# Final norm of a state-space plus expert block: who gathers, who normalises, and in which buffers, during the last expert

## The chip, the cores and the metric

The kernel runs on one core of one Trainium2 chip. The metric is the device time of one execution in microseconds, as a median of several. Engines: TensorE (PE, with its weight loads PEld), VectorE (DVE), ScalarE (ACT), GpSimd (POOL), and SyncE (SP), which here only issues DMAs. Each engine works through its own list of instructions in order and waits on semaphores.

## The reference, cut to what matters

```python
x = L0_attn_hidden_states                        # 8 x 2048 x 256, so 16384 tokens of 256
x = _layernorm(x + attn(x, ...))                 # a state-space layer, stages 1 and 2
x = _layernorm(x + ffn(x, ...))                  # this case: the end of the ffn and this layernorm

def ffn(x, gate_w, ln_w, ln_b, fc1s, b1s, fc2s, b2s):
    xf = x.reshape(-1, 256)
    scores = softmax(xf @ gate_w.T)              # 8 experts
    vals, idx = top_k(scores.T, 2048)            # each expert picks its 2048 tokens
    y = xf[flat_idx]                             # gathered rows
    y = (y - mu) * rsqrt(var + 1e-5) * ln_w + ln_b
    h = gelu(y @ fc1 + b1)                       # 256 -> 1024
    out = (h @ fc2 + b2) * kept_w                # 1024 -> 256
    xf = xf.at[flat_idx].add(out)                # scatter-add
```

The last layernorm has no weights. It needs each token's sum over all experts that picked the token.

## The kernel before, in words

Stages 1 and 2 (the state-space layer, the gate and the top-k) are not touched. Stage 3 works through 8 experts, each in 4 groups (t = 0 to 3) of 512 tokens. For one group, POOL gathers 512 rows with four indirect DMAs (`gather`, L1524), VectorE takes their statistics, POOL makes rstd and shift (`rstd_and_shift`, L1538), ScalarE normalises into `xn` (`normalise`, L1661), TensorE turns `xn` (`turn`, L1750), and then computes the first layer (8 slices m of 128 hidden units, PE L1779) and the second layer (L1801, L1802, L1807). ScalarE's gelu writes each slice twice (`hraw`, `hidden_upper`, L1696); VectorE subtracts the two (`hidden_rest`, `rest_of_hidden`, L1446). `hraw` is a ring of 4 slices, so the gelu of slice m waits for the hidden_rest of slice m - 4. TensorE starts a first-layer slice only when the gelu of the slice two before is done. The result, weighted, is added to the tensor `sums` in memory by indirect DMA.

In the last expert nothing is added to `sums`. Once the scatters of expert 6 have landed, SyncE loads `sums` in 16 row tiles of 1 MB (8 rows of 256 on each of 128 partitions, 2048 floats a partition) in `final_rows` (L1483), they are normalised in place and written to `out`. Rows that the last expert picked are written wrong by this and are written again at the very end: POOL gathers the 4 groups of "late" rows from `sums` into the upper part of `xg` (`late_rows`, L1575), VectorE adds the expert's result to them (L1978), and after all 16 row tiles have been written POOL writes the late rows to `out` with 16 indirect DMAs (L1651).

A list `UNITS` (L1402) sets the order in which the 16 row tiles and 4 late tiles get their statistics from VectorE (`final_stats`, L1917) and their rstd and shift from POOL (`final_rstd`, L1586): late 0, rows 0 to 2, late 1, rows 3 to 5, late 2, rows 6 to 8, late 3, rows 9 to 15. The norm itself is made by POOL for row tiles 1, 3, 5, 7, 9, 11 and 14, by ScalarE for the other nine (tiles 0 and 2 behind group t = 1, 4 behind t = 2, the rest behind t = 3), and by VectorE for the 4 late tiles (`late_norm`, L1940). VectorE's list for one group t of the last expert (`last_step`, L1949): the 8 hidden_rest with the statistics of one row tile between them, and the statistics of the next group's gathered rows behind slice 5 (t < 2); another row tile and the norm of late t - 1; the second layer's bias; the sum and statistics of late t; one more row tile. POOL's list at t = 0: the last scatter, rstd and shift of group 2, the gathers of group 3, a wait for all scatters, the gathers of late 0, 1 and 2, the rstd of late 0 and of rows 0, rstd and shift of group 3. From t = 1 on it goes through `UNITS`.

The row tiles use 5 buffers of 1 MB in turn, tile k in buffer k mod 5, made from storage that is free by then. SyncE issues the write of tile k when it is normalised and then, when the write of tile k - 1 has landed, the load into its buffer.

Of the kernel before, what the change touches and what calls it, by code (L numbers as in the profile page):

```python
# [22 lines left out]
P = 128  # L23
# [1312 lines left out]
def stage3(nc, d, n_tok):  # L1336
# [11 lines left out]
    with ExitStack() as ctx:  # L1348
# [11 lines left out]
        isin = a.sb("isin", [P, SL, G // 2, 16, 2], BF16)  # L1360
# [6 lines left out]
        xn = a.sb("xn", [P, 4, 256])  # L1367
# [34 lines left out]
        UNITS = [("late", 0), ("rows", 0), ("rows", 1), ("rows", 2), ("late", 1), ("rows", 3), ("rows", 4), ("rows", 5),  # L1402
                 ("late", 2), ("rows", 6), ("rows", 7), ("rows", 8), ("late", 3)] + [("rows", k) for k in range(9, PAIRS)]
        BY_POOL = (1, 3, 5, 7, 9, 11, 14)
        BY_ACT = {1: (0, 2), 2: (4,), 3: tuple(k for k in range(5, PAIRS) if k not in BY_POOL)}
        ACT_PAIRS = [k for t in (1, 2, 3) for k in BY_ACT[t]]
        assert sorted(ACT_PAIRS + list(BY_POOL)) == list(range(PAIRS))
# [3 lines left out]
            onehots[:, 2 * i:2 * i + 2].bitcast(F32).rearrange("p o g t two -> p (o g t two)") for i in range(2)]  # L1411
        NBUF = len(row_bufs)
        late = [x[:, :, 0:256] for x in xg]
# [6 lines left out]
        scored, merged, late_normed = S("score_halved"), S("late_summed"), S("late_normed")  # L1420
        st4, var4, rstd4_ok, shift4_ok = S("stats4_steps"), S("variance4"), S("rstd4_ready"), S("shift4_ready")
        rows_act, rows_pool = S("rows_normed_act"), S("rows_normed_pool")

        def unit(kind, i):

            return UNITS.index((kind, i))

        def row_tile(k):

            return row_bufs[k % NBUF].rearrange("p (r f) -> p r f", r=R)  # L1430

        def rows_normed(k):

            if k in BY_POOL:
                return rows_pool, BY_POOL.index(k) + 1
            return rows_act, ACT_PAIRS.index(k) + 1
# [17 lines left out]
        with nc.Block() as block:  # L1454
# [9 lines left out]
            def _(sp):  # L1464
# [18 lines left out]
                def final_rows():  # L1483

                    def load(k):
                        sp.dma_start(row_bufs[k % NBUF], row_view[k]).then_inc(rows_in[k % NBUF], 16)
# [7 lines left out]
                    for k in range(NBUF):  # L1494
# [163 lines left out]
            def _(act):  # L1658
# [23 lines left out]
                def step(e, t, p, following, later, ahead):  # L1682
# [419 lines left out]
```

## Time and profile before

| | us |
|---|---|
| median of 3 timed runs | 4347.4 (4343.74 to 4348.07) |
| the profiled execution | 4336.49 |
| its span | 4334.7 |
| mean granted TensorE clock over the span | 0.935 of full speed |

The page's busy shares over the whole span are PE 82%, DVE 86%, ACT 80%, POOL 82%. The page cuts the span into 40 slices of 108 us; the last two, in which the rest of this text happens, are much less busy than those before (PE 9 and 2 tenths, DVE 6 and 5, ACT 5 and 6, POOL 5 and 5), while the data moved rises from 64 to 147 and 224 GB/s. To read the rest, take the timelines of the engines over that stretch: each line has a start, a duration, an engine, a line of the kernel and the tiles, and in square brackets how long the engine had been idle and what released it. All times count from the start of the span.

### The profile page before, as it was taken

What the parts mean: (1) busy time and instruction counts of PE and PEld (TensorE: products, weight loads), DVE (VectorE), ACT (ScalarE), POOL (GpSimd) and SP (SyncE); (2) the same over time, 40 slices, a digit from 0 to 9 for tenths busy, and PEclk for the clock granted to TensorE, in tenths of its full rate; (3) what the DMA queues carried; (4) which work ended last, traced back from release to release, by engine and by line L of the source; (5) the groups of instructions that cost most, each with busy time, mean ns of one, the idle gap of its engine ahead of it and who ended that gap; (6) DMA issues with size and microseconds to landing.
All of it is one profiled execution on the core that took longest, in us unless ns stands there. A gap on an engine that the chain in (4) does not pass through costs nothing. (4 is left out here: it accounts for less than half of the span.)

```text
span 4334.7 us, 57726 instructions
## 1 busy us (share of the span) xinstructions
PE 3537.5 (82%) x19574; PEld 2468.4 (57%) x19574; DVE 3748.0 (86%) x4812; ACT 3478.0 (80%) x5921; POOL 3543.3 (82%) x1863
## 2 busy tenths in 40 slices
PE   7778888888888888888888888888766499999992
PEld 3455555555555555555555555555555388888872
DVE  5899999999999999999999999999997766566565
ACT  5889999899999999999989999999883256556563
POOL 3899999999999999999999999999894255555565
PEclk9999999999999999999999999999986699999996
DMA  2667776776667677677767666667674133333345
GB/s 85 152 159 171 173 169 165 171 175 163 164 160 165 161 176 170 169 174 167 167 166 175 163 166 163 162 161 171 158 164 77 57 72 64 64 60 65 64 147 224
DMA packets 178854, 628.41 MB, mean 145 GB/s; under 512 B 33648, under 2 KB 97264, under 8 KB 119168
## 3 DMA queue, kind: packets, MB, share of 16 engines
q0 software_dynamic: 73920, 368.61, 42.3%
q1 hardware_dynamic: 104640, 256.10, 17.6%
q8 instruction: 157, 2.57, 0.2%
q14 instruction: 137, 1.12, 0.1%
HBM read 223.57 MB, written 68.68 MB: 67 GB/s over the span
## 5 line engine op out<-in xcount | busy, mean ns | idle before, releaser
L463 POOL TENSOR_TENSOR dbu<-du,bb 128x2048 f32<-128x2048 f32 x511 | 2432.3, 4813 | 103.0 <-DVE h L939 78.0
L939 DVE TENSOR_TENSOR_SCAN h<-da,hlast,dbu 128x512 f32<-128x512 f32 x1536 | 1867.5, 1265 | 76.8 <-POOL dbu L463 51.0
L791 PE MATMUL ht<-ident,h 128*128 128x128 f32 x8192 | 1170.9, 287 | 458.3 <-DVE h L939 174.3
L524 ACT ACTIVATE da<-dl,negA 128x512 f32<-128x512 f32 x2048 | 1414.1, 702 | 118.9 <-DVE h L939 113.4
L791 PEld LDWEIGHTS ht<-ident,h 128*128 128x128 f32 x8192 | 959.5, 146 | 872.4 <-DVE h L939 317.2
L543 ACT ACTIVATE pair<-ht,ct 128x512 f32<-128x512 f32 x896 | 592.7, 689 | 127.1 <-PE ht L791 68.6
L939 DVE TENSOR_TENSOR_SCAN h<-da,dbu 128x512 f32<-128x512 f32 x512 | 592.5, 1204 | 45.0 <-POOL dbu L463 24.2
L715 PE MATMUL spare<-xin,win 128*128 128x512 f32 x1024 | 495.3, 614 | 11.8 <-DMA xin<-in_xt 7.3
L724 PE MATMUL spare<-xh,conv 128*128 128x512 f32 x1024 | 464.6, 596 | 0.9 <-ACT xh L555 0.8
L1696 ACT ACTIVATE hraw<-f,b 128x512 f32<-128x512 f32 x256 | 176.5, 689 | 262.3 <-PE f L1779 236.6
L447 POOL DMA_DIRECT2D acc<-pair x222 | 227.3, 1024 | 143.5 <-ACT pair L543 60.7
L1560 POOL DMA_INDIRECT sums<-ot,idx x112 | 178.1, 1590 | 158.5 <-DVE ot L2038 132.9
L724 PEld LDWEIGHTS spare<-xh,conv 128*128 128x128 f32 x1024 | 184.3, 190 | 190.8 <-issue 187.1
L543 ACT ACTIVATE acc<-ht,ct 128x512 f32<-128x512 f32 x384 | 264.7, 702 | 27.9 <-PE ht L791 20.4
L947 DVE SCALAR_TENSOR_TENSOR acc<-ht,ct,acc 128x512 f32<-128x512 f32 x384 | 270.7, 732 | 13.7 <-PE ht L791 12.7
L947 DVE SCALAR_TENSOR_TENSOR pair<-ht,ct,pair 128x512 f32<-128x512 f32 x384 | 276.8, 728 | 2.9 <-PE ht L791 2.9
L715 PEld LDWEIGHTS spare<-xin,win 128*128 128x128 f32 x1024 | 182.2, 195 | 161.7 <-issue 154.6
L1448 DVE TENSOR_TENSOR hidden_rest<-hraw,hidden_upper 128x512 fp32r<-128x512 f32 x256 | 172.8, 687 | 96.4 <-ACT hidden_upper L1696 96.4
L1801 PE MATMUL f<-w_upper,hidden_upper 128*128 128x256 f32 x1024 | 250.4, 283 | 0.0
L1802 PE MATMUL f<-w_rest,hidden_upper 128*128 128x256 f32 x1024 | 247.9, 281 | 0.0
L761 PE MATMUL spare<-wo,g 128*128 128x256 f32 x992 | 231.1, 387 | 1.7 <-ACT du L585 1.2
L1779 PE MATMUL f<-yt_upper,w_upper 128*128 128x512 f32 x512 | 215.2, 420 | 16.6 <-ACT hidden_upper L1696 13.5
(241 smaller groups left out, 5678.0 us busy)
## 6 DMA issues: line engine op xcount, KB each, us to landing
acc<-pair POOLq DMA_DIRECT2D x222, 1024.0 KB, 7.3
bb<-b_rows SPq DMA_DIRECT2D x128, 1024.0 KB, 6.3
acc<-acc POOLq DMA_DIRECT2D x64, 1024.0 KB, 7.8
dl<-du POOLq DMA_DIRECT2D x62, 512.0 KB, 5.9
x_scores<-scores_and_rows SPq DMA_DIRECT2D x33, 512.0 KB, 4.5
xin<-in_xt SPq DMA_DIRECT2D x32, 512.0 KB, 4.9
sums<-scores_and_rows SPq DMA_DIRECT2D x32, 512.0 KB, 6.2
scores_and_rows<-in_x SPq DMA_DIRECT2D x31, 512.0 KB, 3.9
```

The source lines that it names most:

```text
L447: pool.dma_start(acc[q][:], sum_tile(q, t)[:], accum_op=ALU.add).then_inc(acc_in, 16)
L463: pool.tensor_tensor(dbu[n % 2][:], du[q][:], bb[part % 2][:, m:m + 1, :].to_broadcast([P, DT, CH]), ALU.mult).then_inc(dbu_done, 1)
L524: act.activation(da[DA_SLOT[m]][:], dl[q][:, dt, :], ACT.Exp, scale=negA[:, dt, n:n + 1]).then_inc(exp_done, 1)
L543: act.mul(target(q, n, b)[:, b, :], ht[HT_SLOT[n * NB + b]][:], ct[q][:, b, n:n + 1]).then_inc(scaled, 1)
L715: last = te.matmul(bank[:], win[:, k, col:col + P], xin[f % 2][:, k, :], start=k == 0, stop=k == 1)
L724: last = te.matmul(bank[:], conv[:, i, k, :], xh[:, i, k:k + CH], start=k == 0, stop=k == 3)
L761: last = te.matmul(bank[:, b * 256:(b + 1) * 256], g[:, k, t0:t0 + P], wo[:, k, :], start=k == 0, stop=k == DT - 1)
L791: last = te.transpose(ht[HT_SLOT[m]][:, dt * P:(dt + 1) * P], h[n % 2][:, dt, b * P:(b + 1) * P], ident[:])
L939: dve.tensor_tensor_scan(h[n % 2][:, dt, :], da[DA_SLOT[n * DT + dt]][:], dbu[n % 2][:, dt, :], start, ALU.mult, ALU.add).then_inc(scan_do ...
L947: dve.scalar_tensor_tensor(part, ht[HT_SLOT[n * NB + b]][:], ct[q][:, b, n:n + 1], part, ALU.mult, ALU.add).then_inc(mac_done, 1)
L1801: te.matmul(out, hbh[:, m, rows], w2h[p][:, m, :], start=m == 0, stop=False)
L1802: te.matmul(out, hbh[:, m, rows], w2l[p][:, m, :], start=False, stop=False)
```

## The change

Eight edits, all in stage 3:

1. POOL gathers late 0 before the gathers of group 3; late 1 and late 2 are gathered after rstd and shift of group 3; late 3 still after late 1's rstd. Rows 0's rstd comes behind those gathers.
2. The order in `UNITS` is the same, but is now built by a rule.
3. VectorE no longer takes a row tile behind the sum of the late rows. In group t it takes tile 3t - 3 among the hidden_rest, 3t - 2 behind them and 3t - 1 between the two halves of the bias. Behind late 3 it takes tiles 9 to 15.
4. `late_norm` of VectorE is gone; ScalarE normalises the late tiles (4 instructions each) in its `final_norm`.
5. ScalarE's list is rows 0 and late 0 behind t = 1, rows 3 and late 1 behind t = 2, rows 6, late 2 and late 3 and the shared tiles behind t = 3. POOL has rows 1, 2, 4, 5, 7, 8 whole.
6. Row tiles 9 to 15 are shared: rows 0 to 3 of each partition by ScalarE, 4 to 7 by POOL.
7. A sixth 1 MB buffer is made of `isin` and `xn`, which become one allocation of the same size. It is first used for tile 7 after TensorE has turned the last group; the order of buffers is `ROW_BUF`.
8. SyncE waits for both engines for a shared tile, and POOL's waits at the end follow the new lists.

```diff
-        isin = a.sb("isin", [P, SL, G // 2, 16, 2], BF16)
+        isin_xn = a.sb("isin_and_xn", [P, 2, 1024])
+        isin = isin_xn[:, 0].bitcast(BF16).rearrange("p (s g n two) -> p s g n two", s=SL, g=G // 2, two=2)
+        xn = isin_xn[:, 1].rearrange("p (b f) -> p b f", b=4)
...
-        UNITS = [("late", 0), ("rows", 0), ("rows", 1), ("rows", 2), ("late", 1), ("rows", 3), ("rows", 4), ("rows", 5),
-                 ("late", 2), ("rows", 6), ("rows", 7), ("rows", 8), ("late", 3)] + [("rows", k) for k in range(9, PAIRS)]
-        BY_POOL = (1, 3, 5, 7, 9, 11, 14)
-        BY_ACT = {1: (0, 2), 2: (4,), 3: tuple(k for k in range(5, PAIRS) if k not in BY_POOL)}
-        ACT_PAIRS = [k for t in (1, 2, 3) for k in BY_ACT[t]]
-        assert sorted(ACT_PAIRS + list(BY_POOL)) == list(range(PAIRS))
+        UNITS = [x for t in range(NG) for x in [("rows", 3 * t + j - 3) for j in range(3 if t else 0)] + [("late", t)]]
+        UNITS += [("rows", k) for k in range(9, PAIRS)]
+
+        def unit(kind, i):
+
+            return UNITS.index((kind, i))
+
+        SHARED = range(9, PAIRS)
+        BY_ACT = {1: (("rows", 0), ("late", 0)), 2: (("rows", 3), ("late", 1)),
+                  3: (("rows", 6), ("late", 2)) + tuple(x for x in UNITS[unit("late", 3) - 1:] if x[1] in SHARED or x[0] == "late")}
+        ACT_UNITS = [x for t in (1, 2, 3) for x in BY_ACT[t]]
+        POOL_PAIRS = [k for k in range(PAIRS) if k in SHARED or ("rows", k) not in ACT_UNITS]
...
+            isin_xn[:].rearrange("p k f -> p (k f)")]
         NBUF = len(row_bufs)
+        ROW_BUF = ([0, 1, 2, 3, 4] + [0, 1, 5, 2, 3, 4] * 2)[:PAIRS]
+        NTH = [ROW_BUF[:k + 1].count(ROW_BUF[k]) for k in range(PAIRS)]
...
+        def rows_of(k, engine):
+
+            half_of = {"act": range(R // 2), "pool": range(R // 2, R)}
+            return half_of[engine] if k in SHARED else range(R)
...
                     for k in range(PAIRS):
-                        s, v = rows_normed(k)
-                        sp.wait_ge(s, v)
-                        sp.dma_start(out_view[k], row_bufs[k % NBUF]).then_inc(rows_out[k % NBUF], 16)
-                        j = k - 1
-                        if j >= 0 and j + NBUF < PAIRS:
-                            sp.wait_ge(rows_out[j % NBUF], 16 * (j // NBUF + 1))
-                            load(j + NBUF)
+                        if ("rows", k) in ACT_UNITS:
+                            sp.wait_ge(normed_act, ACT_UNITS.index(("rows", k)) + 1)
+                            sp.sem_inc(sp_passed3, 1)
+                        if k in POOL_PAIRS:
+                            sp.wait_ge(normed_pool, POOL_PAIRS.index(k) + 1)
+                        sp.dma_start(out_view[k], row_bufs[ROW_BUF[k]]).then_inc(rows_out[ROW_BUF[k]], 16)
+                        for n in range(5, PAIRS):
+                            if NTH[n] > 1 and k > 0 and ROW_BUF[n] == ROW_BUF[k - 1] and NTH[n] == NTH[k - 1] + 1:
+                                sp.wait_ge(rows_out[ROW_BUF[n]], 16 * NTH[k - 1])
+                                load(n)
+                            if NTH[n] == 1 and k == 2:
+                                sp.wait_ge(tp_ok, 2 * E * NG)
+                                load(n)
...
                 def last_step(t):
 
                     if t == 0:
                         scatter(LAST - 1, NG - 1, 1 - LAST % 2)
                         rstd_and_shift(LAST * NG + 2)
-                        gather(LAST, 3, LAST % 2)
                         for k in range(NG):
                             pool.wait_ge(added[k], 64 * LAST)
-                        late_rows((0, 1, 2))
+                        late_rows(0)
+                        gather(LAST, 3, LAST % 2)
                         final_rstd("late", 0)
-                        final_rstd("rows", 0)
                         rstd_and_shift(LAST * NG + 3)
+                        late_rows(1)
+                        late_rows(2)
                     elif t == 1:
-                        for kind, i in UNITS[2:5]:
+                        for kind, i in UNITS[1:]:
                             final_rstd(kind, i)
-                            if kind == "rows" and i in BY_POOL:
+                            if kind == "rows" and i in POOL_PAIRS:
                                 final_norm(i)
-                        late_rows((3,))
-                        for kind, i in UNITS[5:]:
-                            final_rstd(kind, i)
-                            if kind == "rows" and i in BY_POOL:
-                                final_norm(i)
+                            if (kind, i) == ("late", 1):
+                                late_rows(3)
...
                 for b in range(NBUF):
-                    pool.wait_ge(rows_out[b], 16 * ((PAIRS - 1 - b) // NBUF + 1))
+                    pool.wait_ge(rows_out[b], 16 * ROW_BUF.count(b))
                 pool.sem_inc(pool_passed, 1)
                 for t in range(NG):
-                    pool.wait_ge(late_normed, t + 1)
+                    pool.wait_ge(normed_act, ACT_UNITS.index(("late", t)) + 1)
                     for b in range(4):
                         pool.indirect_dma_start(
                             out=d["out"], out_offset=bass.IndirectOffsetOnAxis(
@@ -1702,17 +1710,17 @@
                     if ahead >= 2:
                         normalise(grp + 2, (t + 2) % NG)
                     if e == LAST:
-                        for k in BY_ACT.get(t, ()):
-                            final_norm(k)
-
-                def final_norm(k):
-
-                    x, tile = unit("rows", k), row_tile(k)
+                        for kind, i in BY_ACT.get(t, ()):
+                            final_norm(kind, i)
+
+                def final_norm(kind, i):
+
+                    x, tile = unit(kind, i), row_tile(i) if kind == "rows" else late[i]
                     act.wait_ge(shift4_ok, x + 1)
-                    for r in range(R):
+                    for r in rows_of(i, "act") if kind == "rows" else range(4):
...
-                    inner = 3 * t - 2
+                    inner = 3 * t - 3
                     for m in range(FM):
                         rest_of_hidden(dve, m, grp)
                         if m == 5 and t < 2:
@@ -1962,13 +1961,14 @@
                     dve.tensor_scalar(score[:, t, :], xg[t][:, :, 256 + e], 0.5, None, ALU.mult).then_inc(scored, 1)
                     if t > 0:
                         final_stats("rows", inner + 1, range(R))
-                        late_norm(t - 1)
                     if t < 2:
                         dve.wait_ge(added[t + 2], 64 * e)
                     for i in range(2):
                         dve.wait_ge(f2_ok, grp * 4 + 2 * i + 2)
                         dve.tensor_tensor(ot[t % 2][:, 2 * i:2 * i + 2, :], f2[i][:].rearrange("p (b f) -> p b f", b=2),
                                           b2[:, bass.ds(e, 1), :].to_broadcast([P, 2, 256]), ALU.add).then_inc(biased, 1)
+                        if i == 0 and t > 0:
+                            final_stats("rows", inner + 2, range(R))
                     dve.wait_ge(biased, 2 * grp + 2)
                     dve.sem_inc(dve_passed, 1)
                     dve.wait_ge(scored, t + 1)
@@ -1979,11 +1979,8 @@
                                                         late[t][:, b, :], ALU.mult, ALU.add)
                     last.then_inc(merged, 1)
                     final_stats("late", t, range(4))
-                    final_stats("rows", 3 * t, range(R))
                     if t == 3:
-                        final_stats("rows", 10, range(R))
-                        late_norm(3)
-                        for k in range(11, PAIRS):
+                        for k in range(9, PAIRS):
```

## Rows read from the trace of the kernel before

**Rows 1.** busy time by stretch: PE, PEld, DVE, ACT, POOL busy (instructions), clock, DMA share, GB/s.
```profile
4168.10:4192.00 23.90, 16.69 (x71) 12.69 (x70) 16.62 (x56) 10.97 (x18) 16.38 (x19) 0.79 0.39 137
4184.00:4188.00 4.00, 3.69 (x9) 2.92 (x10) 4.00 (x10) 2.14 (x5) 1.34 (x2) 0.50 0.02 4
```

**Rows 2.** PE in order of time: start, us, what, count, idle before and its releaser.
```profile
4143.97 0.39 PE L1779 MATMUL f<-yt_upper,w_upper 128*128 128x512 f32 x1
...
4168.10 0.39 PE L1779 MATMUL f<-yt_upper,w_upper 128*128 128x512 f32 x1
...
4184.31 0.80 PE L1779 MATMUL f<-yt_upper,w_upper 128*128 128x512 f32 x1 [7.21 <-ACT hidden_upper L1696]
...
4189.59 1.04 PE L1759 MATMUL tp<-ident,xn 128*128 128x128 f32 x8
...
4207.54 0.51 PE L1779 MATMUL f<-yt_upper,w_upper 128*128 128x512 f32 x1 [2.76 <-ACT hidden_upper L1696]
...
4216.50 0.38 PE L1759 MATMUL tp<-ident,xn 128*128 128x128 f32 x2
...
4228.73 0.39 PE L1779 MATMUL f<-yt_upper,w_upper 128*128 128x512 f32 x1
```

**Rows 3.** DVE in order of time.
```profile
4174.94 1.67 DVE L1978 SCALAR_TENSOR_TENSOR xg<-ot,score,xg 128x256 f32<-128x256 f32 x4 [5.95 <-DMA xg<-sums,idx]
...
4178.65 2.70 DVE L1928 BATCH_NORM_STATS2 stats<-scores_and_rows 128x6 f32<-128x256 f32 x8
...
4182.22 1.28 DVE L1448 TENSOR_TENSOR hidden_rest<-hraw,hidden_upper 128x512 fp32r<-128x512 f32 x2
...
4187.13 1.40 DVE L1854 BATCH_NORM_STATS2 stats<-xg 128x6 f32<-128x256 f32 x4
...
4221.83 2.69 DVE L1928 BATCH_NORM_STATS2 stats<-scores_and_rows 128x6 f32<-128x256 f32 x8
...
4290.42 2.71 DVE L1928 BATCH_NORM_STATS2 stats<-scores_and_rows 128x6 f32<-128x256 f32 x8 [1.31 <-DMA scores_and_rows<-sums]
```

**Rows 4.** ACT in order of time.
```profile
4182.99 0.69 ACT L1696 ACTIVATE hraw<-f,b 128x512 f32<-128x512 f32 x1 [7.60 <-DVE hidden_rest L1448]
...
4193.60 2.09 ACT L1667 ACTIVATE xn<-xg,shift,rstd 128x256 f32<-128x256 f32 x4
4195.57 4.06 ACT L1713 ACTIVATE scores_and_rows<-scores_and_rows,shift,rstd 128x256 f32<-128x256 f32 x8
...
4206.25 0.67 ACT L1696 ACTIVATE hraw<-f,b 128x512 f32<-128x512 f32 x1
```

**Rows 5.** POOL in order of time.
```profile
4166.36 0.95 POOL L1581 DMA_INDIRECT xg<-sums,idx  x1 [0.30 <-issue]
...
4180.31 0.95 POOL L1581 DMA_INDIRECT xg<-sums,idx  x1 [0.30 <-issue]
...
4182.91 2.08 POOL L1590 TENSOR_TENSOR rstd<-ve,half 128x8 f32<-128x8 f32 x1
...
4191.62 0.22 POOL L1550 TENSOR_TENSOR shift<-nmean,rstd 128x4 f32<-128x4 f32 x1
...
4216.58 6.23 POOL L1600 TENSOR_SCALAR onehots<-onehots,rstd,shift 128x256 f32<-128x256 f32 x8
...
4227.68 5.15 POOL L1600 TENSOR_SCALAR scores_and_rows<-scores_and_rows,rstd,shift 128x256 f32<-128x256 f32 x8
...
4289.19 1.64 POOL L1590 TENSOR_TENSOR rstd<-ve,half 128x8 f32<-128x8 f32 x1 [5.41 <-DVE ve L1938]
...
4291.21 4.34 POOL L1600 TENSOR_SCALAR onehots<-onehots,rstd,shift 128x256 f32<-128x256 f32 x8
```

**Rows 6.** DMA issues, us to landing: from 4155 to 4190, then to the end.
```profile
xg<-x_scores,idx POOLq DMA_INDIRECT x4, 6.1
...
onehots<-sums SPq DMA_DIRECT2D x4, 1024.0 KB, 8.7
```

**Rows 7.** chain of work that ended last: start, us, what.
```profile
4301.53 3.84 DMA out<-scores_and_rows
```

More of the change, by code:

```diff
@@ L1410, in stage3 @@
         row_bufs = [d["wide"], wraw[:], rhs[:].bitcast(F32).rearrange("p s g a t two -> p (s g a t two)")] + [
-            onehots[:, 2 * i:2 * i + 2].bitcast(F32).rearrange("p o g t two -> p (o g t two)") for i in range(2)]
+            onehots[:, 2 * i:2 * i + 2].bitcast(F32).rearrange("p o g t two -> p (o g t two)") for i in range(2)] + [
+            isin_xn[:].rearrange("p k f -> p (k f)")]
         NBUF = len(row_bufs)
+        ROW_BUF = ([0, 1, 2, 3, 4] + [0, 1, 5, 2, 3, 4] * 2)[:PAIRS]
+        NTH = [ROW_BUF[:k + 1].count(ROW_BUF[k]) for k in range(PAIRS)]
         late = [x[:, :, 0:256] for x in xg]
@@ L1573, in prologue, with late_rows @@
                     rstd_and_shift(1)
-                def late_rows(some):
-                    for t in some:
-                        pool.wait_ge(xn_ok, LAST * NG + t + 1)
-                        pool.sem_inc(pool_passed, 1)
-                        for b in range(4):
-                            pool.indirect_dma_start(
-                                out=late[t][:, b, :], out_offset=None, in_=d["acc"],
-                                in_offset=bass.IndirectOffsetOnAxis(
-                                    ap=idx[LAST % 2][:, 4 * t + b:4 * t + b + 1], axis=0)).then_inc(late_in[t], 16)
+                def late_rows(t):
+                    pool.wait_ge(xn_ok, LAST * NG + t + 1)
+                    pool.sem_inc(pool_passed, 1)
+                    for b in range(4):
+                        pool.indirect_dma_start(
+                            out=late[t][:, b, :], out_offset=None, in_=d["acc"],
+                            in_offset=bass.IndirectOffsetOnAxis(
+                                ap=idx[LAST % 2][:, 4 * t + b:4 * t + b + 1], axis=0)).then_inc(late_in[t], 16)
                 def final_rstd(kind, i):
@@ L1923, in final_stats @@
                         if kind == "rows":
[L1924 removed]
+                            dve.wait_ge(rows_in[ROW_BUF[i]], 16 * NTH[i])
                         else:
@@ L1938, in final_stats @@
                     dve.tensor_scalar(ve4[:, x, 0:n], mv4[:, x, 0:n, 1], LN_EPS / 4, None, ALU.add).then_inc(var4, 1)
-                def late_norm(t):
-                    x = unit("late", t)
-                    dve.wait_ge(shift4_ok, x + 1)
-                    for b in range(4):
-                        last = dve.tensor_scalar(late[t][:, b, :], late[t][:, b, :], rstd4[:, x, b:b + 1],
-                                                 shift4[:, x, b:b + 1], ALU.mult, ALU.add)
-                    last.then_inc(late_normed, 1)
                 def last_step(t):
                     grp, e = LAST * NG + t, LAST
-                    inner = 3 * t - 2
+                    inner = 3 * t - 3
                     for m in range(FM):
```

26 lines of the change are left out of this document (9 added, 17 removed).

## Prediction, made before the changed kernel was timed

> **What bounds the kernel now.** The page first: the diff touches only the last expert's four groups of tokens (t = 0 to 3) and the final norm, which lie from about 4144 us to the end at 4334.7, some 190 us of the span. So I read only that stretch. The chain that ended last comes next: it ends in the write of row tile 15 at 4301.53 [rows 7], and everything behind it is fixed: 3.84 us for the write, then 16 indirect writes of late rows. From that write's issue to the end of the span it is 4334.7 - 4301.53 = 33.2 us. The question is therefore: when can the write of tile 15 be issued?
>
> Going back, the timelines of the engines show three stops of TensorE. (1) In t = 1: VectorE waits 5.95 us for the gathered late rows of group 0, sums them, then takes the statistics of row tile 0, and only at 4182.22 starts the hidden_rest work that the ring of hidden buffers needs [rows 3]; ScalarE stood 7.60 us [rows 4] and TensorE 7.21 us [rows 2], and after it the array's granted clock was 0.50, its 1.2 GHz level, in the stretch from 4184 to 4188 [rows 1]: 12 matmuls took 4189.59 - 4184.31 = 5.28 us. (2) In t = 2: ScalarE normalises row tiles 0 and 2 before it returns to the gelu at 4206.25 [rows 4], and TensorE stood 2.76 us [rows 2]. (3) In t = 3 a smaller one, again VectorE's late tile. An undisturbed group takes 4168.10 - 4143.97 = 24.13 us [rows 2]; turn and second layer are 4228.73 - 4216.50 = 12.23 of it, so the first layer is 11.90.
>
> **The change, part by part.** All times are on the axis of the profiled span.
>
> *Late rows of group 0 gathered first.* Four gathers leave POOL's queue ahead of the four of group 3. They take the slots that the others had: the first late gather stood at 4166.36 [rows 5], each four cost about 5 us at (4180.31 - 4166.36)/11 = 1.27 us apiece, so the last now goes at about 4165.1. They meet the first 5 MB of row loads; gathers in these slots took 6.1 us to land [rows 6]. Arrival: 4165.1 + 6.1 = 4171.2 instead of 4174.94, 3.7 us earlier. I do not take the full 5.
>
> *Tile 0's statistics leave VectorE's path.* One tile costs 4182.22 - 4178.65 = 3.57 us [rows 3]. Hidden_rest then starts at 4171.2 + (4182.22 - 4174.94) - 3.57 = 4174.9. ScalarE wants it for its fifth gelu at about 4175.7 (the first layer started at 4168.10 and gives a result about every 1.5 us). So stop (1) vanishes, with its slow matmuls: t = 2 can start at 4168.10 + 24.13 = 4192.2.
>
> *What is late next: POOL's queue.* POOL now does, in order: late rstd 0, rstd and shift of group 3, gathers of late 1 and late 2, and only then the rstd of row tile 0. Before, those gathers stood ahead. Statistics of group 3 started at 4187.13, 12.19 us after the late rows arrived; now 12.19 - 3.57 = 8.6 after 4171.2, 4179.8. Their rstd and shift end 4191.84 - 4187.13 = 4.7 later [rows 3, 5]: 4184.5. Eight gathers: 0.4 + 7 x 1.27 + 0.95 = 10.2, 4194.7. Tile 0's rstd and shift, by the row behind gathers 2.08 and its shift, 2.5: 4197.2. ScalarE has been waiting with the norms of tile 0 and late 0 in front of t = 2's gelu: 4.06 + 2.09 [rows 4] gives 4203.4. TensorE restarts 4207.54 - 4206.25 = 1.3 after that: 4204.7. It ran dry at 4192.2 + 11.90/4 = 4195.2, so it stands 9.5 us: stop (2) grows from 2.8 to 9.5 and eats most of what stop (1) gave. After a stop of 7.2 us the clock was at its low level and 12 matmuls cost 5.28 - 11.90/4 = 2.3 us more; I charge that again. From the restart to t = 3's start it was 4228.73 - 4207.54 = 21.2, now 23.5: t = 3 starts at 4228.2, only 0.5 us earlier than before. The bounds: no fall of the clock -2.3; a gather 0.25 us dearer each would be +2.
>
> The Trainium skill's page "TensorE: Matmul & The Clock Gate" (Part 1) says that the array drops to half rate when it has been idle and gets the full rate back through activity. The trace agrees (0.50 behind the 7.21 us stop). Without that rule and row the sum would be 2.3 us smaller.
>
> *Group 3's stop.* VectorE no longer takes a row tile after the late one of t = 2, so hidden_rest comes 3.57 us sooner than before and ScalarE need not wait. The first layer ends at 4228.2 + 11.9 = 4240.1. ScalarE's own norms (tile 3, late 1) need their shifts by about 4221.5, end at 4227.7 and free it before t = 3's first result at 4229.7.
>
> *VectorE.* Its four late norms go to ScalarE; none of them stood in the chain of the three stops. In t = 2 statistics of the tile after hidden_rest began 4221.83 - 4216.50 = 5.3 after the first layer's end; t = 3 lacks the 1.5 us of yt_rest: 3.8. With 3.57 the variance of tile 7 is there at 4240.1 + 3.8 + 3.57 = 4247.5.
>
> *POOL's last stretch, the new end.* POOL takes 9.5 tiles instead of 7. From tile 7 on it is never idle. Rstd and shift to the norm's start 4291.21 - 4289.19 = 2.02; a norm of 8 rows 4.34, but 5.15 and 6.23 beside VectorE's work [rows 5]. Tile 7 beside the late sum: 2.0 + 5.15; tile 8: 2.0 + 4.4; late 3's rstd: 1.3; seven shared tiles at 2.02 + 4.34/2 = 4.19: 29.3. Sum 44.2, so tile 15 is normalised at 4291.7. ScalarE's half (2.05 a tile) hides beside it. VectorE needs 3.57 a tile and is ahead.
>
> The Trainium skill's "SBUF — State Buffer" (Who interferes with whom) says that GpSimd reads wait for a VectorE instruction with two SBUF inputs, whole instructions long. That fits 6.23 against 4.34, and by it tile 7 could cost 6.2: 1.1 more.
>
> *Loads.* The last load (tile 15) goes after tile 9's write has landed, about 4266.4 + 5 = 4271.4 (3.84 alone [rows 7], taken as 5 beside other traffic); with the 8.7 us that loads took late in the trace [rows 6] it lands at 4280.1, VectorE is done by 4283.7, POOL wants it at 4287.5. Before, VectorE did wait for such loads (1.31 at tile 15 [rows 3]). The sixth buffer and the earlier turn hide it with 4 us to spare. The cost taken is 0.
>
> *Sum.* 4301.53 - 4291.7 = 9.8 us less, call it 9.7 with the issue. The profiled execution took 4336.49 us, 1.8 over its span, so by it 4326.8; the median of the timed runs is 4347.4, 10.9 above that execution, and a change in the tail does not touch the difference: 4347.4 - 9.7 = 4337.7.
>
> **Rivals.** What a measurement of this kernel tells from no change is 0.2%, 8.7 us: above 4356.1 is slower, below 4338.7 faster. My 9.7 is close to that edge.
> - *A half norm is not half.* If the shared tiles cost POOL more (both engines in one tile, VectorE's statistics beside them): 5.15/2 instead of 2.17 is +0.4 x 7 = 2.9; with 6.23/2 it is +6.6; with a longer second stop (+2) the end comes at 4341 to 4346. For it: the spread of the three norms [rows 5]. Against: in the tail VectorE does statistics with one input, where 4.34 stood.
> - *The clock does not pay.* The second stop leaves the clock high, as 2.76 us did [rows 2], or ScalarE gets tile 0 earlier: 2.3 to 5 us better, 4333 to 4335.
> - *Slower: the array stays at its low level.* From the restart at 4204.7 through t = 3. The ratio is 5.28/(11.90/4) = 1.77; 21.2 + 23.4 us of array time at 1.77 is +34, less 2.3 counted: some 4369. It starts to lose all of the gain from 12.6 us of array time at the low level on. Against it: the clock came back within about 5 us of restart [rows 1, 2]. For it: the stop is longer than any in this stage now. (The same page of the Trainium skill, Part 1's caveats, reports a clock gate stuck low for long; no run shows it here.)
> - *It does not do what it says.* If late 0 lands no earlier (4174.9), the second stop is 3.7 longer: 4341.4. Against: the slots are 5 us earlier.
>
> **How the numbers follow.** Forecast 0.50 (4334.5 to 4341), half norms and longer stop 0.22, better 0.13, no earlier landing 0.08, clock low 0.04, noise or effects elsewhere 0.03. Faster by over 0.2%: 0.65 of the forecast's half, all of the better case and a little of the rest: 0.50. Slower 0.07, the same 0.43. The range that leaves out 2 in 10 is 4331.5 to 4345.5.
>
> **What would show it.** TensorE without a stop in t = 1 and clock 1.00 there; one stop of 8 to 11 us in t = 2, ended by ScalarE's norm of tile 0 behind POOL's shift; t = 3 starting near 4228 (relative to the last scatter); POOL busy without a gap from tile 7 to tile 15 at about 4.2 us a tile; VectorE never waiting for a load by more than 1 us. I am wrong if the stop in t = 2 is under 5 us, if VectorE or a load releases POOL in the last 30 us, or if a shared tile costs POOL over 5 us.

## The result, and the profile after

The changed kernel took 4328.22 us (median of 6 runs, 4325.21 to 4334.82) beside 4343.07 us for the kernel before (6 runs, 4338.44 to 4348.07): a ratio of 0.9967, 95% interval 0.9954 to 0.998. That is 14.8 us less; 9.7 were forecast, and 4328.2 lies below the range's end of 4331.5. The six runs of the kernel before contain the three that the prediction had, and these are its three highest (4343.74 to 4348.07); the other three took 4338.44 to 4342.41 us. Against those alone the difference would be 10.8 us. Two later comparisons of the same two kernels, with more runs, gave ratios of 0.9979 (0.997 to 0.9988) and 0.9978 (0.9969 to 0.9987), that is 8 to 10 us.

The profiled executions hardly differ in span, 4333.1 us against 4334.7. To read them, the part that the change touches has to be cut out. I count from TensorE's first matmul of t = 0 in the last expert (line 1779 before, 1787 after) to the end of the span and call this *the stretch*. TensorE, after (start us, us, what, idle before it and its releaser):

```profile
4150.84 0.39 PE L1787 MATMUL f<-yt_upper,w_upper 128*128 128x512 f32 x1
...
4174.97 0.39 PE L1787 MATMUL f<-yt_upper,w_upper 128*128 128x512 f32 x1
...
4181.12 0.51 PE L1787 MATMUL f<-yt_upper,w_upper 128*128 128x512 f32 x1 [3.20 <-ACT hidden_upper L1704]
...
4214.22 0.80 PE L1787 MATMUL f<-yt_upper,w_upper 128*128 128x512 f32 x1 [8.58 <-ACT hidden_upper L1704]
...
4236.79 0.40 PE L1787 MATMUL f<-yt_upper,w_upper 128*128 128x512 f32 x1
```

The anchor stood at 4143.97 before [rows 2] and stands at 4150.84 here, 6.9 us later, behind work that is the same in both kernels. The stretch is 4334.7 - 4143.97 = 190.7 us before and 4333.1 - 4150.84 = 182.3 after: some 8.5 less. TensorE's stop of 7.21 us in t = 1 [rows 2] is 3.20 here (none in two later profiles of the same kernel), and in t = 2 there is one of 8.58 where 2.76 stood. Behind it the granted clock was 0.50 (in these busy times by stretch, the first number behind the five counts), the 1.2 GHz level, as it was behind the 7.21:

```profile
4204.00:4212.00 8.00, 1.42 (x6) 0.69 (x4) 4.40 (x15) 4.98 (x11) 7.66 (x10) 0.90 0.13 39
4212.00:4216.00 4.00, 1.78 (x4) 1.49 (x5) 1.35 (x3) 3.31 (x7) 3.92 (x6) 0.50 1.00 416
```

Who made the stop is in ScalarE's timeline: it stood 10.30 us for POOL's shift of row tile 0, then made the norms of tile 0 and late 0:

```profile
4207.02 4.04 ACT L1721 ACTIVATE scores_and_rows<-scores_and_rows,shift,rstd 128x256 f32<-128x256 f32 x8 [10.30 <-POOL shift L1602]
4210.96 2.06 ACT L1721 ACTIVATE xg<-xg,shift,rstd 128x256 f32<-128x256 f32 x4
4212.93 0.66 ACT L1704 ACTIVATE hraw<-f,b 128x512 f32<-128x512 f32 x1
```

The end is in POOL's timeline and in SyncE's last write. From tile 7's rstd on POOL has no gap, and a shared tile costs 4276.79 - 4272.64 = 4.15 us; a norm of 4 rows takes 2.16, half of the 4.34 of 8 rows [rows 5]. In the kernel before, the rstd of tile 9 began at 4264.13; in the changed kernel it began at 4270.63:

```profile
4264.13 1.64 POOL L1590 TENSOR_TENSOR rstd<-ve,half 128x8 f32<-128x8 f32 x1 [2.28 <-DVE ve L1938]
```

```profile
4256.20 1.64 POOL L1600 TENSOR_TENSOR rstd<-ve,half 128x8 f32<-128x8 f32 x1 [1.73 <-DVE ve L1946]
...
4270.63 1.64 POOL L1600 TENSOR_TENSOR rstd<-ve,half 128x8 f32<-128x8 f32 x1
...
4272.64 2.16 POOL L1610 TENSOR_SCALAR onehots<-onehots,rstd,shift 128x256 f32<-128x256 f32 x4
4274.77 1.64 POOL L1600 TENSOR_TENSOR rstd<-ve,half 128x8 f32<-128x8 f32 x1
4276.48 0.20 POOL L1602 TENSOR_TENSOR shift<-nmean,rstd 128x8 f32<-128x8 f32 x1
4276.79 2.16 POOL L1610 TENSOR_SCALAR onehots<-onehots,rstd,shift 128x256 f32<-128x256 f32 x4
...
4297.52 2.16 POOL L1610 TENSOR_SCALAR onehots<-onehots,rstd,shift 128x256 f32<-128x256 f32 x4
```

```profile
4299.70 0.33 SPq L1507 DMA_DIRECT2D out<-onehots  x1
```

The last write is issued 148.9 us into the stretch; before it was 4301.53 - 4143.97 = 157.6 [rows 7]. Behind it stand 33.4 us, before 33.2. Nearly the whole gain lies in the last seven tiles: from tile 9's rstd to the last write it is 4301.53 - 4264.13 = 37.4 us before and 4299.70 - 4270.63 = 29.1 after, 8.3 less.

### The profile page after: what moved, and what is told of

It is laid out like the page before. It is cut to its first block and busy times, and to the rows that moved or that the text cites. A ratio compares the mean times of both kernels' runs of the same rounds, so it can differ in the third digit from the quotient of the medians.

```text
span 4333.1 us, 57736 instructions
## 1 busy us (share of the span) xinstructions
PE 3545.1 (82%) x19574; PEld 2477.0 (57%) x19574; DVE 3741.0 (86%) x4796; ACT 3476.0 (80%) x5917; POOL 3575.5 (83%) x1883
## 5 line engine op out<-in xcount | busy, mean ns | idle before, releaser
L1571 POOL DMA_INDIRECT sums<-ot,idx x112 | 199.5, 1781 | 163.1 <-DVE ot L2035 137.5
```

## The experiments

Each was timed in 5 rounds beside the kernel before and profiled once. The ratios are not always the quotient of the medians (they differ by up to 0.0009, for "balanced, 5 and 3"), so read a ratio with its interval. "Stretch" is from the profile, "last write" the place of its issue in the stretch.

| kernel | median us (before beside it) | ratio, 95% | stretch | last write |
|---|---|---|---|---|
| before, first profile / again | 4336.00 (4336.46) | 0.9998, 0.999 to 1.0007 | 190.7 / 190.2 | 157.6 / 157.1 |
| changed, first profile | 4328.22 (4343.07) | 0.9967, 0.9954 to 0.998 | 182.3 | 148.9 |
| changed, again | 4328.68 (4336.83) | 0.9979, 0.997 to 0.9988 | 181.8 | 148.3 |
| changed, third time | 4326.39 (4336.46) | 0.9978, 0.9969 to 0.9987 | 182.4 | 148.9 |
| rstd of tile 0 early | 4327.79 (4336.83) | 0.9981, 0.9972 to 0.999 | 183.9 | 150.4 |
| tail 5 and 3 rows | 4322.45 (4336.83) | 0.9969, 0.9958 to 0.9979 | 179.7 | 146.2 |
| tail tiles whole | 4327.70 (4336.83) | 0.9981, 0.9972 to 0.999 | 184.2 | 150.7 |
| late 0 gathered second | 4330.34 (4334.72) | 0.9989, 0.998 to 0.9998 | 184.2 | 150.9 |
| five buffers | 4327.76 (4334.72) | 0.9986, 0.9977 to 0.9995 | 183.0 | 149.7 |
| before + sharing | 4328.66 (4334.72) | 0.9988, 0.9979 to 0.9997 | 185.2 | 152.0 |
| order only | 4333.85 (4336.46) | 0.9996, 0.9987 to 1.0004 | 189.5 | 156.2 |
| balanced, 5 and 3 | 4317.82 (4334.72) | 0.9970, 0.9958 to 0.9982 | 174.2 | 140.8 |
| balanced, 4 and 4 | 4319.69 (4333.63) | 0.9966, 0.9954 to 0.9978 | 176.6 | 143.2 |

### The changed kernel again (no edit)

> The changed kernel once more, timed and profiled. In its first profile the stretch from TensorE's first layer of t = 0 in the last expert to the end of the span was 182.3 us (before: 190.7), and inside it ScalarE and VectorE both stood until 4179.8 though TensorE had delivered at about 4177, 3.2 us lost. Theory N (that wait is an accident of one execution): the new stretch is 179.1 us, and the timed ratio stands for 11 to 12 us less. Rival M (the wait belongs to the change, because engines and gathers now meet the five row loads): it appears again with 2 to 5 us, the stretch is 181 to 184 us, and the gain of the tail is only 8 to 9 us, so that the rest of the timed 14.8 comes from elsewhere.

Measured: 8.2 us less by the medians, stretch 181.8. The wait of ScalarE and VectorE did not come again; TensorE ran t = 1 without a stop. But theory N had the size wrong: the stretch is 181.8 and not 179.1, and in a third profile, also without that wait, 182.4. So what happened in the first profile cost at most 0.5 us at the end and not 3.2: without it VectorE waits for late 0 and TensorE's next stop is longer. VectorE's and TensorE's rows of this second profile:

```profile
4175.86 1.67 DVE L1978 SCALAR_TENSOR_TENSOR xg<-ot,score,xg 128x256 f32<-128x256 f32 x4 [2.89 <-DMA xg<-sums,idx]
```

```profile
4147.92 0.39 PE L1787 MATMUL f<-yt_upper,w_upper 128*128 128x512 f32 x1
...
4209.65 0.79 PE L1787 MATMUL f<-yt_upper,w_upper 128*128 128x512 f32 x1 [9.67 <-ACT hidden_upper L1704]
```

Late 0's sum starts 4175.86 - 4147.92 = 27.9 us into the stretch; before it was 31.0 [rows 3].

### POOL makes tile 0's rstd before the late gathers

```diff
                         rstd_and_shift(LAST * NG + 3)
+                        final_rstd("rows", 0)
                         late_rows(1)
                         late_rows(2)
...
-                            final_rstd(kind, i)
+                            if (kind, i) != ("rows", 0):
+                                final_rstd(kind, i)
```

> The changed kernel with one move: POOL makes the rstd and shift of row tile 0 before it gathers late 1 and late 2, not behind them. Theory: TensorE's stop in t = 2 (8.6 us) is POOL's queue: 8 gathers of 1.25 us each stand before the shift that ScalarE needs. With the move ScalarE starts tile 0's norm about 8 us sooner, the stop falls to 0 to 2 us and the clock stays up (1.4 us); the time falls by 7 to 9 us, unless POOL's chain at the end takes part of it back (it can't: it starts from tile 7's variance, which moves along). Rival: ScalarE's 6.1 us of norms are the stop, then it falls by less than 3 us. Second rival: late 1 now lands too late for VectorE's sum (needed some 13 us after the shift, the gathers take 5 + 3), then VectorE waits and t = 3 gets the stop.

Measured: nothing gained (0.9981 beside the changed kernel's 0.9979), stretch 1.8 us longer. The stop in t = 2 did go, as the theory said, but it came back in t = 3. ScalarE, TensorE and one norm of POOL in this kernel:

```profile
4223.27 4.04 ACT L1723 ACTIVATE onehots<-onehots,shift,rstd 128x256 f32<-128x256 f32 x8 [14.57 <-POOL shift L1602]
```

```profile
4230.47 0.79 PE L1789 MATMUL f<-yt_upper,w_upper 128*128 128x512 f32 x1 [10.72 <-ACT hidden_upper L1706]
```

```profile
4199.65 8.17 POOL L1610 TENSOR_SCALAR wraw<-wraw,rstd,shift 128x256 f32<-128x256 f32 x8
```

ScalarE now waits 14.57 us for the shift of tile 3, which stands behind everything that POOL has to do between: 8 gathers, two norms, 4 more gathers. One of the norms, tile 1's, now falls beside VectorE's hidden_rest and took 8.17 us; in the changed kernel it took 4.42. Taking one wait away showed that the bound is not that wait but POOL's queue. I had written that POOL's chain could not take the gain back; it did.

### The last seven tiles, 5 rows to ScalarE and 3 to POOL

```diff
-            half_of = {"act": range(R // 2), "pool": range(R // 2, R)}
+            half_of = {"act": range(5), "pool": range(5, R)}
```

> The changed kernel with the shared tiles cut 5 rows to ScalarE and 3 to POOL in place of 4 and 4. Theory: POOL bounds the last 30 us at 4.15 us a tile (rstd and shift 2.0, norm 0.54 a row), so one row less gives 3.6 a tile, and 7 x 0.54 = 3.8 us less, of which VectorE's 3.57 a tile and the last load (its wait of 1.1 us at tile 15) leave 3 to 3.8. Rival (the loads bound the tail): no more than 1 us.

Measured: stretch 179.7, 2.5 us under the mean of the changed kernel's three (182.2); by the medians 6.2 us, which with the spread of single runs (4319.3 to 4325.7 and 4322.4 to 4331.5) says no more than that it is faster. POOL's share does bound the tail, though a little less comes through than forecast: a tile now costs 3.6 us, and the last write is at 146.2.

### The last seven tiles whole

```diff
-        SHARED = range(9, PAIRS)
+        SHARED = ()
+        TAIL_ACT = (10, 12, 13, 15)
...
-                  3: (("rows", 6), ("late", 2)) + tuple(x for x in UNITS[unit("late", 3) - 1:] if x[1] in SHARED or x[0] == "late")}
+                  3: (("rows", 6), ("late", 2)) + tuple(x for x in UNITS[unit("late", 3) - 1:] if x[1] in TAIL_ACT or x[0] == "late")}
```

> The changed kernel with the last seven tiles not shared: POOL normalises 9, 11 and 14 whole and ScalarE 10, 12, 13 and 15, as before the change; all else stays, the sixth buffer too. Theory: sharing itself is worth little, since POOL then has 3 x 6.3 + 4 x 1.9 = 26.5 us in place of 29.1, and ScalarE's whole norm of tile 15 adds 4.1 against 2.2: time higher by 0 to 2 us, loads permitting. Rival: sharing is what the change gains by, for it spreads the writes and so the loads evenly; then the time rises by 5 us or more and VectorE waits for loads again as before (5.9 us in all in the last stretch).

Measured: stretch 184.2, 2.0 longer: the theory's upper end. VectorE waited 3.9 us for tile 15's load, but POOL only 0.4 us for VectorE.

### Late 0 gathered behind group 3

```diff
+                        gather(LAST, 3, LAST % 2)
                         late_rows(0)
-                        gather(LAST, 3, LAST % 2)
```

> The changed kernel with one thing undone: POOL gathers group 3 first and late 0 behind it, as before the change. The stretch of the changed kernel, from TensorE's first layer of t = 0 to the end, is 181.8 us. Theory P (POOL is the bound from t = 1 on: it works without a gap from the rstd of group 3 until the rstd of tile 3, and what TensorE loses only moves): VectorE gets late 0 about 2 to 3.5 us later, so POOL's rstd of group 3, which stands behind VectorE's work, and all behind it come 2 to 3.5 us later; stretch 184 to 185. Rival T (the stop of TensorE in t = 1 is what the order gained, 7 us and the clock): stretch 188 or more.

Measured: stretch 184.2, 2.0 longer, theory P's 184 to 185. TensorE had a stop of 3.1 us in t = 1 again and one of 8.6 in t = 2. The stop is not the 7 us of the kernel before, because tile 0's statistics stay out of VectorE's path; what removing all of it is worth is seen further down, in "order only". Gathering late 0 first is worth 2 us.

### Five buffers

```diff
-        ROW_BUF = ([0, 1, 2, 3, 4] + [0, 1, 5, 2, 3, 4] * 2)[:PAIRS]
+        ROW_BUF = [k % 5 for k in range(PAIRS)]
...
-                for b in range(NBUF):
+                for b in range(5):
```

> The changed kernel with five buffers in turn (tile k in buffer k mod 5) instead of six. The load of tile k then waits for the write of tile k - 5: tile 14 for tile 9's, at 123.3 us of the stretch, tile 15 for tile 10's, issued at 127.4; they were loaded after tiles 8 and 9. Theory: VectorE's wait for the last tile grows from 2.8 to about 7 us, and as POOL needs tile 15's variance 3.5 us after it is there now, the stretch grows by 3 to 5 us to 185 to 187. Rival: the sixth buffer is worth nothing (under 1 us), because POOL and not the loads is the bound of the tail.

Measured: stretch 183.0, 0.8 longer. The expectation was too dear, the rival is nearer: VectorE waits 5.9 us for four loads instead of 1.1 to 3.2 in the three profiles of the changed kernel, but it is so far ahead of POOL that POOL stands only 0.4 us (tile 14) and 1.0 us (tile 15) for it.

### The kernel before with the sharing alone

```diff
-        BY_POOL = (1, 3, 5, 7, 9, 11, 14)
-        BY_ACT = {1: (0, 2), 2: (4,), 3: tuple(k for k in range(5, PAIRS) if k not in BY_POOL)}
+        SHARED = tuple(range(9, PAIRS))
+        BY_POOL = (1, 3, 5, 7) + SHARED
+        BY_ACT = {1: (0, 2), 2: (4,), 3: (6, 8) + SHARED}
...
-                    for r in range(R):
+                    for r in range(R // 2 if k in SHARED else 0, R):
...
-                    for r in range(R):
+                    for r in range(R // 2 if k in SHARED else R):
```

The first loop is POOL's norm, the second ScalarE's; SyncE waits for both engines for a shared tile.

> The kernel before with the sharing of tiles 9 to 15 alone (rows 0 to 3 ScalarE, 4 to 7 POOL); order, five buffers and VectorE's late norms stay. In the kernel before, the last write goes out at 157.6 us of the stretch and VectorE waits 5.9 us for loads of tiles 13 to 15. Theory: the writes of tiles 9 to 12 come earlier and evenly (every 4.2 us from tile 9's rstd at 120), so the loads do too; the last write goes out at about 150 to 151.5, 6 to 7.5 us sooner, most of the 9 us of the whole change. Rival (five buffers still make the loads the bound): under 3 us. The parts are then not additive, for undoing the sharing alone in the changed kernel cost 2.4 us of stretch.

Measured: last write at 152.0 and stretch 185.2, 5.3 under the kernel before (190.5, the mean of two): more than half of the change's 8.3, a little under what was expected.

### Order only: neither sharing nor sixth buffer

```diff
-        SHARED = range(9, PAIRS)
+        SHARED = ()
+        TAIL_ACT = (10, 12, 13, 15)
...
-        ROW_BUF = ([0, 1, 2, 3, 4] + [0, 1, 5, 2, 3, 4] * 2)[:PAIRS]
+        ROW_BUF = [k % 5 for k in range(PAIRS)]
...
-                for b in range(NBUF):
+                for b in range(5):
```

What is left is all the rest of the change: the order of the gathers, VectorE's new places for the tiles, the late norms on ScalarE and the new owners of tiles 0 to 8.

> The changed kernel without sharing and without the sixth buffer: the new order of gathers, VectorE's new places for the tiles, ScalarE's late norms and the new assignment of tiles 0 to 8 are what is left. In the kernel before tile 9's rstd began at 120.2 us of the stretch, in the changed one at 119.0. Theory: all that the new order does for TensorE (stop of 7.2 us gone, another of 9.7 in its place) is worth 1 us at that point, so what is left is within 3 us of the kernel before: stretch 186.5 to 190. With sharing undone alone it was 184.2, with the sixth buffer undone alone 183.0; since both act on the same loads, undoing both should cost more than 2.4 + 1.2. Rival (the parts add): stretch 185.4.

Measured: stretch 189.5 and a ratio of 0.9996 (0.9987 to 1.0004): no difference that can be told from none. The whole new order, with TensorE's long stop of t = 1 gone, brings about 1 us. The parts do not add: sharing and the sixth buffer undone alone cost 2.0 and 0.8, together 7.3. What they share is in VectorE's waits over the last stretch. In the kernel before (us in total, times, longest):

```profile
DVE stats L1928 <- DMA onehots<-sums: 4.6, 2, 3.7
DVE stats L1928 <- DMA scores_and_rows<-sums: 1.3, 1, 1.3
```

order only:

```profile
DVE stats L1937 <- DMA onehots<-sums: 7.2, 2, 3.7
DVE stats L1937 <- DMA scores_and_rows<-sums: 1.5, 1, 1.5
DVE stats L1937 <- DMA rhs<-sums: 0.6, 1, 0.6
```

and the changed kernel, second profile:

```profile
DVE stats L1936 <- DMA onehots<-sums: 2.8, 1, 2.8
DVE stats L1936 <- DMA rhs<-sums: 0.4, 1, 0.4
```

Writes free buffers, loads fill them, and VectorE starts the next tile. Either finer writes (sharing) or one buffer more keeps that loop close to POOL's pace; with neither, tile 15 comes late and POOL waits for its variance. In "order only" that wait is 5.42 us, as it was 5.41 in the kernel before [rows 5]; with the sixth buffer but no sharing it was 0.4, with sharing but five buffers 1.0, and the changed kernel has none:

```profile
4286.30 1.64 POOL L1601 TENSOR_TENSOR rstd<-ve,half 128x8 f32<-128x8 f32 x1 [5.42 <-DVE ve L1947]
```

### The kernel before again, and the changed one a third time

> The kernel before against itself, timed and profiled. What is open is why the timed level moved: 4347.4 in the first runs, 4343.1, 4336.8 and 4334.7 in later ones of the same kernel. Theory D (stages 1 and 2, which the change does not touch, take more or less from execution to execution, and the last 190 us do not): the stretch from TensorE's first layer of t = 0 in the last expert to the end is 190.7 within 0.5, while its start lies anywhere between 4135 and 4151; the ratio is 1 within its interval, which shows how far such a comparison can be trusted. Rival (the stretch itself varies by several us): it differs from 190.7 by 2 us or more.

> The changed kernel a third time. It was 14.8 us faster in the first comparison and 9.1 in the second (by medians), by the stretch of its two profiles 8.5 and 9.0. Theory D: the stretch is 181.8 within 0.5 and the timed difference is 7 to 11 us. Rival (the change also gains 4 to 6 us where it alters nothing, by another placement of its code or data): the difference is 13 us or more, with the stretch at 181.8.

Measured: before against itself 0.9998, and its stretch is 190.2. Its anchor in this execution:

```profile
4141.31 0.39 PE L1779 MATMUL f<-yt_upper,w_upper 128*128 128x512 f32 x1
```

The changed kernel: 10.1 us less by the medians, 0.9978, stretch 182.4. Theory D holds. The stretch of the two kernels that were profiled more than once repeats within 0.6 us, while the anchor, before which all kernels do the same work, lay anywhere from 4135.8 to 4150.8 in the fourteen profiles. The single runs of the kernel before lay between 4328.1 and 4348.1 us. The later comparisons ran on three different chips, but that is not what spreads them: within one of them, on one chip, the kernel before ran from 4328.1 to 4343.9.

### Balanced: what the second experiment pointed to

```diff
-        BY_ACT = {1: (("rows", 0), ("late", 0)), 2: (("rows", 3), ("late", 1)),
+        BY_ACT = {1: (("rows", 0), ("late", 0)), 2: (("rows", 2), ("late", 1)),
```

with tile 0's rstd early and 5 and 3 rows.

> The changed kernel with three moves, drawn from theory P: rstd of tile 0 before the gathers of late 1 and 2; in t = 2 ScalarE takes tile 2 and late 1 and POOL takes tile 3, so that ScalarE waits for nothing that POOL makes late; 5 and 3 rows of the shared tiles. Alone, the first move only carried TensorE's stop of 9.7 us from t = 2 to t = 3 (10.7 us), where ScalarE waited 14.6 us for tile 3's shift behind POOL's queue. Theory P: with no engine waiting for POOL before the tail, TensorE runs its four groups without a stop over 2 us (96 us), POOL stays busy from the rstd of group 3 to the end and ends its last norm at 133 to 138 us of the stretch; stretch 166 to 172, time 10 to 15 us under the changed kernel. Rival (ScalarE's gelu and norms, or the loads, bound it next): the stops go but VectorE waits for loads, stretch 174 to 178. Second rival: no gain at all, the stop moves a third time.

Measured: 4317.82 us, ratio 0.9970 (0.9958 to 0.9982), stretch 174.2: 8 us under the changed kernel and 16 under the kernel before, less than the 10 to 15 hoped for. (The two ratios, 0.9970 here and 0.9978 for the changed kernel, have intervals that overlap; it is the stretch that tells the two apart.) TensorE has one stop left of more than 1 us, of 1.09, and POOL no idle time of 1 us or more between group 3's rstd and its last norm. VectorE does wait for the loads of five tiles, 7.3 us together, as the first rival said:

```profile
DVE stats L1938 <- DMA scores_and_rows<-sums: 2.5, 1, 2.5
DVE stats L1938 <- DMA onehots<-sums: 1.3, 1, 1.3
DVE stats L1938 <- DMA rhs<-sums: 1.3, 1, 1.3
DVE stats L1938 <- DMA isin_and_xn<-sums: 1.1, 1, 1.1
DVE stats L1938 <- DMA wraw<-sums: 1.1, 1, 1.1
```

But these waits do not set the end: in the last seven tiles POOL stands only 0.57 us for VectorE, before tile 15. POOL's queue is still the bound, and it is longer than hoped because tile 1's norm, which now falls beside VectorE's hidden_rest, takes 8.11 us. At the very end ScalarE's five rows are done 0.9 us after POOL's three:

```profile
4192.54 8.11 POOL L1610 TENSOR_SCALAR wraw<-wraw,rstd,shift 128x256 f32<-128x256 f32 x8
...
4272.01 1.64 POOL L1600 TENSOR_TENSOR rstd<-ve,half 128x8 f32<-128x8 f32 x1 [0.57 <-DVE ve L1948]
```

The same with 4 and 4 rows:

> The balanced kernel with 4 and 4 rows of the shared tiles again, so that only two moves stand against the changed kernel: rstd of tile 0 ahead of the late gathers, and in t = 2 tile 2 for ScalarE and tile 3 for POOL. Stretches so far: changed 181.8 to 182.4, first move alone 183.9, 5 and 3 rows alone 179.7, all three 174.2. Theory P (two engines' queues have to fit; POOL's work before the tail is then unbroken and TensorE stops nowhere for long): the two moves are worth what all three are less the 2.1 to 2.7 of the rows, stretch 176 to 178.5. Rival (the gain was the rows' and the first move's, the exchange of tiles is nothing): 181 or more.

Measured: stretch 176.6, as theory P says. So the early rstd, which alone lost 1.8 us, gains 5.6 together with the exchange of tiles 2 and 3, which takes a norm out of POOL's queue ahead of tile 3's shift and ScalarE's wait for that shift out of t = 2. The exchange without the early rstd was not run.

## Why the prediction was right, and where it was wrong

In the stretch, step by step (the prediction's times less 4143.97; measured in the changed kernel's second profile):

| step | predicted | measured |
|---|---|---|
| late 0 has arrived | 27.2 | 27.9 |
| group 3's shift ready | 40.5 | 41.5 |
| tile 0's shift ready | 53.2 | 54.5 |
| stop of TensorE in t = 2 | 9.5, ends 60.7 | 9.7, ends 61.7 |
| t = 3 starts | 84.2 | 84.9 |
| tile 7's variance, POOL starts on it | 103.5 | 104.4 |
| last write | 147.7 | 148.3 |
| stretch, three profiles | 181.0 | 182.3, 181.8, 182.4 |

- *The stop of t = 1 goes, a larger one comes in t = 2, and t = 3 starts almost where it did.* Right, in place, cause and size. In the three profiles of the changed kernel t = 3 starts at 86.0, 84.9 and 85.5; in the two of the kernel before at 84.8 and 86.2. The forecast for TensorE's whole side of the change was 0.5 us, and the experiment with the order alone gives 1; profiles that differ by up to 1.4 us at this point do not resolve so little. The sign "no stop in t = 1" did not hold in the first profile (3.20 us), but did in the other two.
- *The clock.* The low level (0.50) came, as charged. From restart to t = 3's start 23.2 us were measured against 23.5 predicted, 22.6 in the first profile.
- *POOL's last stretch.* 44.2 us predicted from tile 7's variance; 43.5 in the first profile, 43.9 in the others. For tile 7's norm the prediction held 6.2 us possible, the longest row of before, by the rule of the Trainium skill ("SBUF — State Buffer", Who interferes with whom) that GpSimd's reads and a VectorE instruction with two SBUF inputs exclude each other; it took 4.7 to 5.0, so the nearest row (5.15) was the better guide here. In t = 3, a norm beside VectorE's two-input hidden_rest took 7.60 us, longer than any row of before, and there the trace agrees with the rule. It lay where POOL had slack: behind it POOL stood 1.21 and 1.73 us for VectorE.
- *Loads cost 0.* Right for the end: POOL did not wait for one. VectorE waited 1.1 to 2.8 us at tile 15, more than the 1 us that the prediction allowed.
- *What failed is the last step of the sum, the level.* I took 4347.4, a median of three runs, for the time of the kernel before, added the tail's change to it, and drew the range from the bounds of the tail alone. In five comparisons that kernel's median was 4343.1, 4336.8, 4334.7, 4336.5 and 4333.6. Of the 4337.7 - 4328.2 = 9.5 us between forecast and result, 4.3 are this level (4347.4 against 4343.1 in the same comparison); the other 5.1 are a difference of 14.8 where 9.7 were forecast, and the next point is on them. The profiled execution, 10.9 us under the three runs, had shown that executions differ by more than the change is worth; I wrote that the difference is not touched by the tail, which is true, and forgot that it is not constant either. With 4336.5 as the level the same forecast gives 4326.8, and the changed kernel measured 4326.4 beside it.
- *The size of the first comparison,* 14.8 us, is not explained by the stretch (8.3). Its interval (8.7 to 20) holds the 9.1 and 9.5 that the later ratios give. Without the three early runs of the kernel before it would be 10.8. That the rest is chance is the simplest reading, and three profiles and two further comparisons agree with it; it was not shown for those very runs, so this part of the miss stays open.
- *The rivals.* The half norm is half (2.16 against 4.34). The clock did not stay low. Late 0 did arrive earlier. None of them was needed.
- *What the prediction did not see* is which part earns what. It ran one chain and found its end about right, but the chain hides that sharing alone is worth 5.3 us and the order alone 1, and that sharing and the sixth buffer each stand in for the other. Added one after another, sharing, order and buffer bring 5.3, 2.2 and 0.8 us of stretch (190.5, 185.2, 183.0, 182.2); order, buffer and sharing bring 1.0, 5.3 and 2.0 (190.5, 189.5, 184.2, 182.2). What a part is worth depends on what is there already.

## What to carry to other kernels

A stop of one engine that is ended by another's in-order queue moves when it is removed, unless work leaves the queue: look at what the waiting engine gets next from the same queue before counting the gain. Where a change touches the last 5% of a kernel, measure and predict that stretch from an anchor in the trace, and take the spread of the level over executions, not the bounds of the edit, for the width of the range. When two measures feed the same loop (here buffers and finer writes), undo them one at a time and together; alone each looked like 1 to 2 us, together they were 7. And a wait of one engine says what bounds the end only if the engine behind it waits too: in the balanced kernel VectorE waited 7.3 us and POOL 0.57.

## What was not expected of the hardware

In the first profile of the changed kernel ScalarE and VectorE both stood in t = 1 and went on within 0.1 us of each other, released by nothing that the profile can name. Both wait there for the same signal (lines 1697 and 1967), that of TensorE's last second-layer matmul of t = 0. That group of matmuls, the first line here, ended at 4175.1:

```profile
4174.02 1.11 PE L1815 MATMUL f<-w_upper,hidden_rest 128*128 128x256 f32 x8
```

```profile
4179.73 0.69 DVE L1968 TENSOR_TENSOR ot<-f,b 128x512 f32<-128x512 f32 x1 [9.48 <-remote]
...
4206.87 0.69 DVE L1968 TENSOR_TENSOR ot<-f,b 128x512 f32<-128x512 f32 x1 [3.11 <-remote]
```

```profile
4179.81 0.69 ACT L1704 ACTIVATE hraw<-f,b 128x512 f32<-128x512 f32 x1 [10.03 <-remote]
```

So both engines went on 4.6 us after TensorE had finished; in the second profile VectorE went on less than 0.1 us after it. The same came once more at 4206.87, 4.4 us after the end of t = 1's second layer. The first time, the five row loads kept the DMA engines full (share 1.02, 403 GB/s from 4176 to 4180); the second time they were mostly idle (39 GB/s from 4204 to 4212), and in the other profiles full DMA engines brought no such wait. Full DMA engines alone are therefore not what makes it, and its cause stays open.

The second surprise is the clock behind short stops of TensorE. Behind one of 2.67 us in "before + sharing" it was at the low level (0.50 from 4211.9 to 4216); behind one of 3.20 us in the first profile of the changed kernel it stayed high (1.00 from 4181 to 4185), as behind the 2.76 us of the kernel before. The length of a stop alone did not tell which it would be:

```profile
4211.99 0.80 PE L1780 MATMUL f<-yt_upper,w_upper 128*128 128x512 f32 x1 [2.67 <-ACT hidden_upper L1697]
```

The third is the spread: the part of the program ahead of the last expert's groups took between 4135.8 and 4150.8 us in fourteen profiles, and the kernel before alone ran from 4328.1 to 4348.1 us.
